# Cross-attention and expert layer on one core: second SiLU, last weight rest, head casts and the opening in another order

## What is computed

```python
# x (8, 256, 128), ctx (8, 256, 96); 1 shared and 8 routed experts
q  = layernorm(x) @ Wq.T;  k = ctx @ Wk.T;  v = ctx @ Wv.T
sim = q @ k.T                       # per batch, 256 x 256
sim = (sim - mean(sim)) * rsqrt(var(sim) + EPS)      # mean, var over the whole matrix
x  = x + softmax(sim) @ v @ Wo.T
h  = layernorm(x)
p  = softmax(h @ gate_w + gate_b);  cw = p where p is in the top 2, else 0
swiglu(z) = silu(z[:, :128]) * z[:, 128:]
x  = x + swiglu(h @ sw1 + sb1) @ sw2 + sb2
       + sum_e cw[:, e] * (swiglu(h @ rw1[e] + rb1[e]) @ rw2[e] + rb2[e])
```

## Time and profile before

| | |
|---|---|
| median of 3 runs | 136.34 us (136.23 to 136.54) |
| the profiled execution, its own time | 136.62 us |
| its span, first to last instruction | 134.8 us |
| busy: PE, PEld | 128.0 us (95%), 97.3 us (72%) |
| busy: DVE, ACT, POOL | 109.6 us (81%), 85.9 us (64%), 23.9 us (18%) |
| granted TensorE clock | 1.00 throughout |
| DMA | 12.97 MB, 96 GB/s on the mean |

### The profile page before, as it was taken

The page is one execution under the profiler, slowest core; times in us unless marked ns, Lnnn a source line. Parts: engine busy times, 40 slices in busy tenths (PEclk is TensorE's granted clock), DMA queues, the critical chain, the costliest instruction groups (busy, mean ns, idle before and its releaser), DMA issues.

```text
span 134.8 us, 2141 instructions
## 1 busy us (share of the span) xinstructions
PE 128.0 (95%) x633; PEld 97.3 (72%) x633; DVE 109.6 (81%) x314; ACT 85.9 (64%) x167; POOL 23.9 (18%) x41
## 2 busy tenths in 40 slices
PE   7999997989999999999999999999899999999992
PEld 7677795748586676688688776688577767787862
DVE  1397788677999999899958998599897888979872
ACT  1547979995547359957673279956742987746240
POOL 7175154056350020500400020000300000000000
PEclk9999999999999999999999999999999999999999
DMA  4999400003900000079000002088000105910022
GB/s 117 299 345 248 139 7 0 0 2 106 354 12 0 0 5 2 5 202 398 22 5 0 0 0 78 5 282 345 5 0 0 54 28 171 401 51 0 5 78 78
DMA packets 8829, 12.97 MB, mean 96 GB/s; under 512 B 1322, under 2 KB 6995, under 8 KB 8307
## 3 DMA queue, kind: packets, MB, share of 16 engines
q1 hardware_dynamic: 8242, 12.62, 27.5%
q10 hardware_dynamic: 576, 0.23, 0.7%
HBM read 11.73 MB, written 1.11 MB: 95 GB/s over the span
## 4 chain that ended last, share of the span: by engine, by line
issue 42%; PE 38%; POOL 9%; DVE 5%; ACT 3%; POOLq 1%; DVEq 0%
PE bank L976 34%; POOL row_powers L399 3%; POOL w_rest L423 3%; POOL ln_rstd L408 2%; ACT prob L497 2%; POOLq L51 1%; POOL sim_r L414 1%; PE bank L992 1%; PE bank L1070 1%; DVE x L884 1%; ACT xn L523 1%; PE bank L1161 1%; DVE act_rest L872 1%; PE bank L1163 0%; PE bank L1040 0%
## 5 line engine op out<-in xcount | busy, mean ns | idle before, releaser
L577 ACT ACTIVATE silu<-bank,b_cols 128x512 f32<-128x512 f32 (+1 forms) x37 | 24.9, 676 | 24.5 <-PE bank L976 24.0
L976 PE MATMUL bank<-x_head,w_head 128*128 128x512 f32 x72 | 33.7, 469 | 0.2 <-issue 0.2
L976 PE MATMUL bank<-x_head,w_rest 128*128 128x512 f32 x72 | 28.6, 397 | 0.0
L976 PE MATMUL bank<-x_rest,w_head 128*128 128x512 f32 x72 | 28.5, 395 | 0.0
L863 DVE SCALAR_TENSOR_TENSOR act<-bank,b_cols,silu 128x512 f32<-128x512 f32 (+1 forms) x34 | 24.8, 733 | 1.9 <-ACT silu L577 1.0
L855 DVE TENSOR_TENSOR silu<-silu,cw_all 128x512 f32<-128x512 f32 (+1 forms) x28 | 18.6, 668 | 2.8 <-ACT silu L577 2.5
L976 PE MATMUL bank<-act,w_sb 128*128 128x512 f32 x36 | 18.4, 592 | 0.0
L976 PEld LDWEIGHTS bank<-x_head,w_head 128*128 128x128 f32 x72 | 13.6, 189 | 5.5 <-issue 2.6
L976 PEld LDWEIGHTS bank<-x_rest,w_head 128*128 128x128 f32 x72 | 13.6, 189 | 3.9 <-issue 1.9
L976 PEld LDWEIGHTS bank<-x_head,w_rest 128*128 128x128 f32 x72 | 13.5, 188 | 3.3
L872 DVE TENSOR_TENSOR act_rest<-act,act_head 128x512 fp32r<-128x512 f32 x16 | 10.7, 686 | 2.0 <-ACT act_head L569 1.9
(11 more groups left out here) (130 smaller groups left out, 222.1 us busy)
## 6 DMA issues: line engine op xcount, KB each, us to landing
cw_all<-cw_dram SPq DMA_DIRECT2D x4, 1024.0 KB, 6.8
cw_all<-cw_dram SPq DMA_DIRECT2D x4, 512.0 KB, 4.8
cw_all<-cw_dram SPq DMA_DIRECT2D x6, 256.0 KB, 3.6
x_sb<-in_x_dram SPq DMA_DIRECT2D x4, 256.0 KB, 4.1
w_sb<-in_L_ffn_rw_dram SPq DMA_DIRECT2D x1, 1024.0 KB, 7.0
ctx_sb<-in_ctx_dram SPq DMA_DIRECT2D x4, 192.0 KB, 4.1
out_dram<-x SPq DMA_DIRECT2D x3, 256.0 KB, 2.1
w_sb<-in_L_ffn_rw_dram SPq DMA_DIRECT2D x1, 512.0 KB, 6.8
```

The lines of the kernel that those rows point to most:

```text
L577: scalar.activation(silu[:, k, cols], hid(n, 0)[:, cols], ACT.Silu, bias=b1_cols[:, 0, e:e + 1]).then_inc(silu_sb, 1)
L976: return pe.matmul(dst, lhs, rhs, start=start, stop=stop, skip_group_check=True)
```

## The change

```diff
         OPENING = {...
-                   ("transpose_cw", 0), ("cw_copy", 0)}
+                   ("transpose_cw", 0), ("cw_copy", 0), ("attend", 1)}
...
-        DIVIDED = [n for n in range(NX - 1, LAST - STRAIGHT) if n >= NX * (C - 1) or n % NX in ((0, 1, 2, 7, 8) if n < NX * 2 else (0, 1, 7, 8))]
-        def divided_in(n):
-            return [m for m in (n - 2, n - 1) if m in DIVIDED and m == (n - 1 if m % NX == 0 or m >= CLOSE_FROM else n - 2)]
+        DIVIDED = [n for n in range(NX - 1, LAST - STRAIGHT)
+                   if n >= NX * (C - 1) or n % NX in ((0, 1, 2, 7, 8) if n < NX * 2 else (0, 7, 8))]
+        def parts_slot(m):
+            return m + 1 if m >= CLOSE_FROM or m % NX in (0, 2) else m + 2
+        def parts_place(m):
+            if m >= CLOSE_FROM:
+                return "between"
+            return {7: "first", 2: "last"}.get(m % NX, "between")
+        def divided_in(n, places):
+            return [m for m in range(n - 2, n) if m in DIVIDED and parts_slot(m) == n and parts_place(m) in places]
...
# gpsimd
-                if n == 3:
+                if n == 2:
                     w1_rests(3)
...
# scalar, opening
             x_copy(2)
+            scalar.wait_ge(small_in, 16 * 3)
+            scalar.wait_ge(setup_ps, 3)
+            scalar.wait_ge(simavg_ps, 2)
+            copy(b1_cols[:, :, :].rearrange("p h e -> p (h e)"), bank[0][:, N - 2 * NX:N]).then_inc(setup_sb, 1)
             ctx_copy(2)
             first_chunk_normalise(range(0, IB))
             v_copy(1)
             x2_heads(0, 0)
-            first_chunk_normalise(range(IB + 1, TC))
             v_copy(2)
             x2_heads(0, 1)
-            scalar.wait_ge(small_in, 16 * 3)
-            scalar.wait_ge(setup_ps, 3)
-            copy(b1_cols[:, :, :].rearrange("p h e -> p (h e)"), bank[0][:, 0:2 * NX]).then_inc(setup_sb, 1)
             u_copy(2)
             exponentials(1)
             router_exp(0)
             expert_silu(0, 0)
+            expert_silu(0, 1)
             cw_copy(0)
...
# scalar, position n
-                if n >= 1:
+                for m in divided_in(n, ("first",)):
+                    act_heads(m)
+                if n >= 2:
                     expert_silu(c, e)
-                for m in divided_in(n):
+                for m in divided_in(n, ("between",)):
                     act_heads(m)
...
+                for m in divided_in(n, ("last",)):
+                    act_heads(m)
...
# vector
             def scores_variance(c):
                 dve.wait_ge(simavg_ps, c + 1)
+                if c == 1:
+                    dve.wait_ge(setup_sb, 3)
...
             scores_variance(1)
-            second_shift(0, 1)
-            dve.tensor_scalar(xn[:, IB, :], x1[:, IB, :], ln_mv[:, 1, IB, 0:1], ln_rstd[:, IB:IB + 1],
-                              ALU.subtract, ALU.mult).then_inc(xn_tile_sb, 1)
+            dve.wait_ge(ln_r[1], 2)
+            dve.wait_ge(xn_ready, 1)
+            for i in range(IB, TC):
+                last = dve.tensor_scalar(xn[:, i, :], x1[:, i, :], ln_mv[:, 1, i, 0:1], ln_rstd[:, i:i + 1], ALU.subtract, ALU.mult)
+            last.then_inc(xn_ready, 1)
...
# tensor, opening
             attend_group(0, 1)
+            pe.wait_ge(small_in, 16 * 3)
+            for h in range(2):
+                last = pe.transpose(bank[0][:, N - (2 - h) * NX:N - (1 - h) * NX], b1_rows[:, h * FF:(h + 1) * FF], ident[0:NX, 0:NX])
+            last.then_inc(setup_ps, 1)
             scores_average(1)
...
# tensor, position n
                 hidden(c, e, 0)
+                if n == 2:
+                    attend(1)
```

More of the change, by code:

```diff
@@ L156, in xattn_moe_kernel @@
         ln_var, ln_r, xn_ready = [sem("ln1_var"), sem("ln2_var")], [sem("ln1_r"), sem("ln2_r")], sem("xn_ready")
-        shift_sb, xn_tile_sb = sem("shift_sb"), sem("xn_tile_sb")
+        shift_sb = sem("shift_sb")
         xt_ps, xt_sb, ctxt_ps, ctxt_sb = sem("xt_ps"), sem("xt_sb"), sem("ctxt_ps"), sem("ctxt_sb")
@@ L526, in normalise @@
             def normalise(c, g):
-                scalar.wait_ge(shift_sb, upto(c, g))
+                scalar.wait_ge(shift_sb, c + 1)
                 scalar.wait_ge(x2t_ps, done(c - 1))
@@ L957, in between @@
                 def between():
-                    for m in divided_in(n):
+                    for m in divided_in(n, ("first", "between")):
                         act_rests(m)
@@ L965, in _ @@
                     expert_gate(c, e, between)
+                for m in divided_in(n, ("last",)):
+                    act_rests(m)
                 if n == 0:
@@ L1065, in transpose_x2 @@
                 pe.wait_ge(xn_ready, upto(c, g))
-                if c == 0 and g == 1:
-                    pe.wait_ge(xn_tile_sb, 1)
                 pe.wait_ge(x1_ready, upto(c, g))
@@ L1214, in _ @@
             project_v(1)
+            project_v(2)
             transpose_x2(0, 0)
[L1216 to L1221, removed]
+            project_u(2)
             transpose_x2(0, 1)
-            project_u(2)
             router(0)
             pe.wait_ge(setup_sb, 3)
+            pe.wait_ge(simavg_sb, 2)
             def transpose_inputs(c):
```

## The result

| | before | changed |
|---|---|---|
| median | 136.44 us (136.23 to 136.76, 4 runs) | 135.16 us (135.09 to 135.37, 4 runs) |
| ratio to before | | 0.9906, 95% interval [0.9887, 0.9925] |
| measured a second time | 136.47 | 135.63 (6 runs), ratio 0.9940 [0.9920, 0.9961] |
| span of the profiled execution | 134.8 us | 133.4 us |

The change makes the kernel faster by 1.3 us by the first measurement and by 0.8 by the second. The forecast was 134.9 (134.3 to 135.9). Some sets hold one or two executions in a slower state (137.8 us and more), which count in the medians given here and not in the ratios.

What follows compares the result with a forecast made beforehand. The prediction took PE's stream of work (busy 95% of the span) plus its holes as the bound. Terms of 0.8 + 0.3 + 0.3 = 1.4 us, taken off the profiled execution and set against the median, gave 134.9 us (134.3 to 135.9).

Steps and rivals of the forecast that it cites:

- Term 1: At hidden(4, 0): DVE's residual of chunk 1 and scale of SiLU 2 start earlier; 0.8 us, bounds 0.5 and 0.85.
- Term 2: Last weight rest ahead of GpSimd's power: DVE's shift shortens, PE's logits wait at 47.31 goes; 0.3 us, bounds 0 and 0.4.
- Term 3: Position 19 undivided: PE's wait at 97.00 goes, chunk 3's transposes start earlier; 0.3 us, bounds 0.1 and 0.5.
- The opening on PE and ACT: First chunk: u copy and SiLU 0 about 0.6 us earlier, so SiLU 1 delays the gate copies only about 0.03 us.
- attend(1): hidden(2, 0) ahead of PE's wait at 30.58: hidden(2, 1) gains 0.79 us, bounds 0.61 and 0.79.
- rival 4: GpSimd's moved weight rest blocks DVE's ln_veps or scale 2; hidden(4, 0) loses 0.1 to 0.8 us: 135.0 to 135.7; chance 0.06.
- Head and rest of 16, 25 and 11: Hole at 87.98 goes, given back at hidden(22, 1): 16 0 (0 to 0.2), 25 0, 11 0 (-0.1 to 0).

Runs made afterwards that it cites:

- a4: The kernel before with attend(1) moved behind hidden(2, 0) and SiLU 1 ahead of the gate copies, opening as before: ratio 0.9996 to the kernel before.
- a1: The kernel before with attend(1) alone moved behind hidden(2, 0): ratio 0.9990 to the kernel before.
- c2: The kernel before with the new opening alone, attend(1) at its old place: ratio 1.0014 to the kernel before.
- b1: The changed kernel with attend(1) back behind hidden(1, 1): ratio 1.0030 to the kernel before.
- a2: The kernel before with the last weight rest alone moved ahead of the power on GpSimd: ratio 0.9999 to the kernel before.
- a3: The kernel before with position 19 alone undivided, one float32 product in place of three passes: ratio 0.9973 to the kernel before.
- b2: The changed kernel with the power ahead of the last weight rest again on GpSimd: ratio 0.9952 to the kernel before.
- c3: The changed kernel with DVE's wait for SiLU 18 behind the rest of 16 (likewise 25 and SiLU 27): ratio 0.9900 to the kernel before.
- b3: The changed kernel with the casts of 16 and 25 behind their SiLU again: ratio 0.9912 to the kernel before.
- c4: The changed kernel with the casts of 16 and 25 behind SiLU again, 11's at its old place, 16 undivided: 134.60 us, ratio 0.9873 to the kernel before.

## Why the prediction was right, and where not

The time and the sign hold, and so do the waits that terms 1 to 3 name. The sizes of terms 1 and 2 were off in opposite directions, term 2 lacked the condition on which it hangs, and the reason given for 16 was wrong.

- **The opening on PE and ACT: right.** The u copy starts at 22.83 against 23.80. Taking off the 0.29 us between the two zeros that is 0.68, against the 0.6 taken. SiLU 0 and 1 run as a pair from 27.05, and the gate copies start at 28.50, which is 28.79 by before's zero: 0.02 later, 0.03 was said. a4 shows the cover at work: without the early opening the gate copies start 0.55 us later by the common zero, where the prediction's sentence says 0.69.
- **attend(1): right at its place** (0.77 of 0.79 at hidden(2, 1), no hole before it).
- **Term 1: 0.59 in place of 0.8, inside its bounds.** The step that was mis-sized is "With the queue ahead of it shorter it does so at about 32.5". By before's zero the residual starts at 32.43 + 0.29 = 32.72. DVE waits for PE there, and it takes the result up 0.35 us after PE's next start (32.08), where I had allowed 0.15. From there on scale and hidden(4, 0) follow as worked out, and hidden(4, 0) is at 36.08 by before's zero, where 35.85 was said. I was also wrong to write as if attend(1) and the opening each brought a part: a1, c2 and a4 give 0.01, -0.01 and 0.07 at hidden(4, 0) and only all of them 0.59. The residual needs a short DVE queue ahead of it (the early SiLU 1) and an input that is not delayed (the opening), and b1, which has both, shows it at its new place without attend(1)'s move. The move is worth PE's own time: in b1 PE's product down ahead of hidden(4, 0) starts at 35.39, so PE is free at 36.25 (0.86 later, see term 2), which is 0.3 us earlier than in the kernel before by the common zero. That is my estimate of what the opening and the early SiLU 1 would bring without the move and without b1's collision; no run has that pair alone.
- **Term 2: 0.56 in place of 0.3, and its step was unsafe.** "Ahead of the power, the rest runs from about 33.4 to 35.2" was right for the change (33.05 to 34.88, by before's zero 33.34 to 35.17), but I had named no condition for it. The condition is ACT's cast behind SiLU 2, which attend(1)'s move makes early. Without it rival 4 comes true: in a2 and b1 ln_veps takes 0.88 and 1.48 us. In the change it gets by with 0.03 us to spare, and that was luck, since nothing in the prediction placed it. On its size: the wait in brackets at 47.31 is 0.26, but the distance from hidden(6, 1) to hidden(7, 0) shrank from 2.21 to 1.70 us, and hidden(6, 0) gained 0.06. The bracket counts from the shown end of the product before, and the product down is shown as 1.02 us where the next start follows after 0.86 (45.08 to 45.94 in the changed kernel, without a wait), so the bracket is short by 0.16. The other 0.07 are in the average itself: hidden(7, 0) follows it after 0.21 us behind the wait and after 0.14 without one.
- **Rival 4, and the rule beside it.** ln_veps (a2, b1) and the shift (the kernel before, a1, a3, a4, b2, c2) were held to the end of GpSimd's weight rest in every run where they met it. The Trainium skill ("SBUF — State Buffer", section "Who interferes with whom") says that an instruction with two inputs in SBUF, or one in a mode that uses both port pairs, as a tensor_scalar from SBUF to SBUF may, is blocked while a GpSimd instruction that started first and reads SBUF is under way, and that one with a single input in SBUF outside those modes is not. For the weight rests the runs agree: in a2 the aggregation, one input, took its 0.38 us within the rest. For GpSimd's powers they disagree, for the same kinds of VectorE instructions kept their length beside a power that had started first. In the kernel before a shift of the first chunk, two inputs in SBUF:

```profile
21.66 0.69 POOL L414 TENSOR_TENSOR sim_r<-sim_veps,minus_half 128x2 f32<-128x2 f32 x1
21.72 0.16 DVE L706 SCALAR_TENSOR_TENSOR ln_shift<-ln_mv,ln_rstd 128x2 f32<-128x2 f32 x1 [0.34 <-POOL ln_rstd L408]
```

  and in the changed kernel ln_veps, beside two powers that last from 7.25 to 10.51:

```profile
7.25 3.26 POOL L410 TENSOR_TENSOR row_powers<-ln_veps,powers 128x8 f32<-128x8 f32 x2 [3.50 <-DVE ln_veps L714]
...
8.38 0.17 DVE L714 TENSOR_SCALAR ln_veps<-ln_mv 128x4 f32<-128x4 f32 x1
```

  Why a power does not hold them no run shows. I had no run that showed the blocking of ln_veps and gave it 0.06, which with 0.03 us of room was too little, though it did not happen.
- **Head and rest of 16, 25 and 11: the price was right, the reason was not.** "with its cast ahead of SiLU 18 that hole goes" fell: the hole is there at 86.69, 0.23 us in brackets, since DVE waits for SiLU 18 ahead of the rest (shown by c3). "PE would wait there for what it gained" holds: c3 loses its 0.48 at hidden(22, 1). Against the 0 taken, the casts cost 0.16 (b3), and 11 some 0.08 at hidden(16, 0), inside its bound of 0.1: b3 still has -1.06 there with 11 at its new place, c4 -1.16 with it back.
- **Term 3: right.** From the b2 pass to the transposes it went as written:

```profile
95.21 1.02 PE L998 MATMUL bank<-act,w_sb 128*128 128x512 f32 x2
...
96.14 0.66 PE L1090 MATMUL bank<-ident,xn 128*128 128x128 f32 x4
```

  The price of the product was set too high: the prediction held a shown 1.02 against a distance between starts of 0.79. By the distance alone the product takes 0.86 us where nothing behind it waits (94.52 to 95.38 in c4) and the three passes 0.77, so it costs 0.09 and not 0.15 to 0.23. The 0.93 in the rows above hold a wait for the normalised tiles, which ACT ends at 96.08. The change gains 0.30 from hidden(22, 1) to hidden(23, 0), a3 alone 0.35, and chunk 3's router takes 0.1 of it back, as "room for 0.3, hardly for 0.6" had it.
- **The sum.** 0.59 + 0.56 + 0.30, less 0.08, 0.09 and 0.13 lost by hidden(16, 0), by hidden(22, 1) and behind hidden(23, 0), is 1.15, where 1.4 was said. Two errors of opposite sign (0.2 and 0.26) hid each other, and the losses were not in the sum.

## What to carry to other kernels

Ask of a gain at a hole which engine's queue stands next, and test edits in pairs: here the opening and attend(1) were worth next to nothing by themselves, and so was attend(1) with the early SiLU; the weight rest lost 0.1 alone and brought 0.56 in company. Before an operation of GpSimd is moved, follow what releases it back to the edit that makes that early or late, and list the small VectorE instructions in its new window. Price a hole by the distance between the starts around it, not by the bracket.

## What the runs showed of the hardware

- A VectorE instruction of 4 elements a partition was held for as long as 1.48 us (ln_veps in b1) by a GpSimd subtraction of 1.83 us, until that ended, while the residual with one operand from PSUM kept its 1.13 us beside it. Beside a GpSimd power of 1.65 us (7.25 to 8.90 in the changed kernel) the same ln_veps kept its 0.17.
- PE's first product of u and x starts anywhere from 6.90 to 7.76 us, though no edit touches what stands ahead of it. Part is the arrival of weights: the product that waits for them starts between 4.49 and 4.95. Part is PE's pace behind it: a3 and the kernel before start that product at 4.66 and 4.62, but four products of ctx and qk later are shown as 1.47 and 1.13 us, and the zeros are 0.38 us apart. The granted clock reads 1.00 in both. The whole of 0.86 us is five times what b3 had to show, so traces have to be brought to one zero before they are compared.
- Where PE waits for one input, more is lost than the bracket says: at 86.69 the bracket is 0.23 us, the distance from the start before (86.07) less the usual 0.23 is 0.39, and with the hole removed c3 is 0.48 us earlier. Most of what is still missing is in the product behind the wait: its next start follows after 0.31 us (86.69 to 87.00), and after 0.24 in c3.
